# The causal mask of the score bank: written by ScalarE in place of an identity matmul, with the slot order of four engines rewritten

## The reference, cut to what matters

```python
mask = (it < jb) | (it > jb + w) | (jb == -1)
sim = jnp.einsum('bhwie,bhwje->bhwij', bq, bk2) * QK_SCALE
sim = jnp.where(mask, -jnp.finfo(sim.dtype).max, sim)
attn = jax.nn.softmax(sim, -1)
out = jnp.einsum('bhwij,bhwje->bhwie', attn, bv2)
```

## Time and profile before

| what | value |
|---|---|
| median of 3 runs | 3747.72 us (3747.24 to 3754.5) |
| the profiled execution, its own time | 3743.95 us |
| its span | 3742.1 us |
| PE busy | 3470.4 us (93%) |
| PE weight loads busy | 2773.6 us (74%) |
| DVE busy | 3141.4 us (84%) |
| ACT busy | 2271.7 us (61%) |
| POOL busy | 1852.4 us (50%) |

### The profile page before, as it was taken

How to read it: one execution, slowest core, us unless ns; L and a number is a source line. 1 busy time by engine, 2 the same in 40 slices (tenths; PEclk the granted TensorE clock), 3 DMA queues, 4 the chain that set the end, 5 groups by cost and what they waited for, 6 DMA issues and landing times.

```text
span 3742.1 us, 161812 instructions
## 1 busy us (share of the span) xinstructions
PE 3470.4 (93%) x63907; PEld 2773.6 (74%) x63907; DVE 3141.4 (84%) x6016; ACT 2271.7 (61%) x4159; POOL 1852.4 (50%) x1604
## 2 busy tenths in 40 slices
PE   5758999999999999999999999999999999999996
PEld 2326787877788878788878788877788887788784
DVE  8987888888788888788888788888788888888883
ACT  2014666666666666666666666666566666666663
POOL 2435455454554554545554445545455445455541
PEclk9988999999999999999999999999999999999998
DMA  2002423323333323333223333232432332332332
GB/s 84 9 28 50 104 60 70 77 54 78 91 67 77 72 56 80 82 77 77 64 64 76 85 77 71 57 77 67 95 72 59 73 77 54 79 74 60 70 77 73
DMA packets 186363, 261.00 MB, mean 70 GB/s; under 512 B 31670, under 2 KB 89908, under 8 KB 185396
## 3 DMA queue, kind: packets, MB, share of 16 engines
q1 hardware_dynamic: 186164, 258.24, 30.7%
HBM read 22.30 MB, written 4.19 MB: 7 GB/s over the span
## 4 chain that ended last, share of the span: by engine, by line
PE 71%; issue 13%; DVE 7%; POOL 3%; ACT 3%; SPq 2%; DMA 1%; ACTq 0%; POOLq 0%; DVEq 0%
PE bank L653 9%; PE bank L705 8%; PE bank L637 7%; PE bank L613 6%; PE obank L687 6%; PE bank L738 5%; PE bank L615 4%; PE bank L614 4%; PE bank L697 4%; PE bank L663 4%; PE bank L745 3%; DVE xs_lo L1139 3%; PE bank L647 2%; PE bank L628 2%; PE bank L630 2%
## 5 line engine op out<-in xcount | busy, mean ns | idle before, releaser
L951 POOL TENSOR_TENSOR qn<-qn,rinv 128x512 f32<-128x512 f32 x768 | 805.4, 1065 | 1382.1 <-DVE rinv L1198 1382.1
L945 POOL TENSOR_TENSOR qn<-ropec,ropes 128x512 f32<-128x512 f32 x768 | 982.9, 1294 | 274.6 <-DVE ropes L1150 230.8
L1149 DVE TENSOR_TENSOR ropec<-bank,rots 128x512 f32<-128x512 f32 x768 | 526.7, 686 | 116.0 <-ACT sq L833 63.7
L1158 DVE TENSOR_REDUCE ss<-sq 128x8 f32<-128x512 f32 x768 | 513.2, 679 | 88.0 <-ACT sq L833 82.6
L1150 DVE TENSOR_TENSOR ropes<-bank,rots 128x512 f32<-128x512 f32 x768 | 523.7, 682 | 0.0
L833 ACT ACTIVATE sq<-bank 128x512 f32<-128x512 f32 x768 | 448.8, 598 | 87.7 <-PE bank L615 68.9
L855 ACT ACTIVATE Pr<-Pr 128x512 f32<-128x512 f32 x384 | 241.9, 630 | 399.1 <-DVE Pr L1209 396.9
L637 PE MATMUL bank<-ident,qn 128*128 128x128 f32 x3072 | 464.1, 274 | 18.4 <-POOL qn L951 14.9
L653 PEld LDWEIGHTS bank<-kT,qT 64*32 64x32 f32 x24576 | 363.1, 107 | 122.0 <-issue 121.9
L613 PE MATMUL bank<-wqkv_hi,xs_hi 128*128 128x512 f32 x768 | 353.1, 460 | 99.2 <-DVE xs_lo L1139 90.8
L637 PEld LDWEIGHTS bank<-ident,qn 128*128 128x128 f32 x3072 | 375.9, 141 | 83.9 <-issue 18.8
(11 more groups left out here) (137 smaller groups left out, 6215.9 us busy)
## 6 DMA issues: line engine op xcount, KB each, us to landing
V<-Vt SPq DMA_DIRECT2D x576, 260.0 KB
V<-Vt SPq DMA_DIRECT2D x192, 130.0 KB
V<-Vt SPq DMA_DIRECT2D x192, 65.0 KB
xres<-X SPq DMA_DIRECT2D x96, 128.0 KB
X<-x SPq DMA_DIRECT2D x96, 128.0 KB, 2.0
wqkv_raw<-L_ffn_Wqkv SPq DMA_DIRECT2D x6, 1536.0 KB
xraw<-X SPq DMA_DIRECT2D x97, 64.0 KB
xraw<-X SPq DMA_DIRECT2D x97, 63.8 KB
```

What stands on the lines that cost most here:

```text
L945: pool.tensor_tensor(qn[:, c, :], ropec[:, c % ROPE_RING, :], ropes[:, c % ROPE_RING, :], ALU.add).then_inc(rope_sum.sem, 1)
L951: pool.tensor_tensor(heads8(qn[:, c, :]), heads8(qn[:, c, :]), rinv[:, 8 * c:8 * c + 8].unsqueeze(2).broadcast_to([P, 8, DH]), ALU.mult).t ...
L1149: dve.tensor_tensor(halves(ropec[:, c % ROPE_RING, :]), raw, table(t, 2 * kind), ALU.mult)
L1158: dve.tensor_reduce(ss[:, 8 * c:8 * c + 8], heads8(sq[:, c % 2, :]), AX.X, ALU.add).then_inc(ss_done.sem, 1)
```

## The change

The mask matmul of each unit is gone. ACT has a step `mk`: it waits for `sim_shift` and writes the mask in float32 from SBUF over the whole bank with a Copy, then counts `mask_put`. PE waits for `mask_put` before the 32 score matmuls, which all add to what is there. One mask matmul is left, once before the pipeline. The order of all four engines is another one.

```diff
@@ ORDER
     "pe": """
-        tr.0' pt.2'' w1.0''' pv.1'' proj.0 proj.1 tr.1' ot.0'' w1.1''' tr.2' pv.2'' pt.3'' tr.3' proj.2
...
+        proj.0 proj.1 tr.2' pt.3'' w1.1''' tr.3' ot.1'' pv.3'' proj.2 proj.3 tr.4' w1.2''' ot.2'' tr.5'
...
@@ tensor
+            pe.matmul(b_sim[:], identb[:], maskb[:, 0, :].unsqueeze(1).broadcast_to([P, 8, 2 * WIN]),
+                      start=True, stop=True).then_inc(sim_begun, 1)
...
-                pe.wait_ge(sim_shift.sem, sim_shift.at(b, u) if u else sim_shift.at(b - 1, 4))
-
-                pe.matmul(b_sim[:], identb[:], maskb[:, 1 if t else 0, :].unsqueeze(1).broadcast_to([P, 8, 2 * WIN]),
-                          start=True, stop=False, skip_group_check=True)
+                hold(pe, pe_held, mask_put.sem, mask_put.at(b, u + 1))
                 for m in range(8):
@@ scalar
+            act.wait_ge(sim_begun, 1)
+
+            def b_mk(b, u):
+                act.wait_ge(sim_shift.sem, sim_shift.at(b, u) if u else sim_shift.at(b - 1, 4))
+                act.activation(heads8(b_sim[:]), mask_f[:, u // 2, :].unsqueeze(1).broadcast_to([P, 8, 2 * WIN]),
+                               ACT.Copy).then_inc(mask_put.sem, 1)
```

More of the change, by code:

```diff
@@ L52 @@
     "pe": """
-        tr.0' pt.2'' w1.0''' pv.1'' proj.0 proj.1 tr.1' ot.0'' w1.1''' tr.2' pv.2'' pt.3'' tr.3' proj.2
-        proj.3 tr.4' ot.1'' w1.2''' tr.5' pv.3'' proj.4 ot.2'' tr.6' w2.0''' ot.3'' tr.7' proj.5 proj.6
-        qk.0' wo.0'' qk.1' proj.7 v.0 mean.0'' pt.0' qk.2' var.0'' pt.1' pv.0' qk.3' v.1 v.2 ln.0'' v.3 """,
+        proj.0 proj.1 tr.2' pt.3'' w1.1''' tr.3' ot.1'' pv.3'' proj.2 proj.3 tr.4' w1.2''' ot.2'' tr.5'
+        proj.4 ot.3'' tr.6' w2.0''' tr.7' proj.5 proj.6 qk.0' wo.0'' qk.1' proj.7 v.0 mean.0'' pt.0' qk.2'
+        v.1 v.2 var.0'' pt.1' pv.0' qk.3' v.3 ln.0'' pt.2' tr.0 pv.1' w1.0'' ot.0' tr.1 pv.2' """,
     "act": """
-        tr.0' xs.0 wa.1 wa.2 qk.3'' w1.0''' pt.2'' proj.0 tr.1' ot.0'' proj.1 w1.1''' tr.2' pt.3'' tr.3'
-        proj.2 proj.3 tr.4' ot.1'' tr.5' w1.2''' wc.2''' ot.2'' proj.4 tr.6' tr.7' ot.3'' proj.5 proj.6
-        qk.0' x1.0'' wc.0'' proj.7 qk.1' v.0 pt.0' mean.0'' qk.2' v.1 pt.1' v.2 ln.0'' wc.1'' v.3 wc.3''' """,
+        xs.0 wa.1 wa.2 tr.0' qk.3'' w1.0''' tr.1' ot.0'' proj.0 proj.1 tr.2' pt.3'' w1.1''' ot.1'' tr.3'
+        mk.0' proj.2 tr.4' proj.3 w1.2''' wc.2''' ot.2'' tr.5' proj.4 tr.6' ot.3'' tr.7' proj.5 proj.6 mk.1'
+        qk.0' x1.0'' wc.0'' proj.7 mk.2' v.0 mean.0'' qk.1' pt.0' v.1 mk.3' qk.2' v.2 pt.1' v.3 ln.0''
+        wc.1'' pt.2' wc.3''' """,
     "dve": """
-        qk.3'' xs.0 wa.1 wa.2 pv.1'' w1.0''' proj.0 proj.1 sums.0 sums.1 pv.2'' w1.1''' proj.2 proj.3 sums.2
-        w1.2''' sums.3 pv.3'' proj.4 sums.4 w2.0''' sums.5 proj.5 sums.6 qk.0' proj.6 x1.0'' qk.1' sums.7
-        mean.0'' proj.7 qk.2' var.0'' rsqrt.0 pv.0' ln.0'' """,
+        xs.0 wa.1 wa.2 pv.2'' w1.0''' sums.0 sums.1 proj.0 proj.1 w1.1''' pv.3'' proj.2 w1.2''' sums.2
+        sums.3 proj.3 proj.4 w2.0''' sums.4 proj.5 qk.0' proj.6 sums.5 sums.6 x1.0'' qk.1' proj.7 mean.0''
+        sums.7 qk.2' var.0'' rsqrt.0 pv.0' ln.0'' qk.3' pv.1' """,
     "pool": """
-        norm.4' norm.5' add.0 add.1 norm.6' add.2 add.3 norm.7' add.4 norm.0 add.5 norm.1 norm.2 norm.3
-        add.6 add.7 """,
+        norm.6' add.0 add.1 add.2 norm.7' add.3 add.4 norm.0 add.5 norm.1 norm.2 add.6 norm.3 norm.4 add.7
+        norm.5 """,
 }
@@ L201, in build @@
         const_in = sem("const_in")
+        sim_begun = sem("sim_begun")
         x_in_sem = [sem(f"x_in_{k}") for k in range(4)]
@@ L251, in build @@
         max_done = per_batch("max_done", 4)
+        mask_put = per_batch("mask_put", 4)
         sim_shift = per_batch("sim_shift", 4)
@@ L894, in c_ln_ @@
                 act.activation(xn[:], lnt[:], ACT.Identity, bias=vec[:, 1:2], scale=vec[:, 0:1]).then_inc(c_xn.sem, 1)
-            steps = {"xs": a_xs, "proj": a_proj, "v": a_v, "tr": a_tr, "qk": b_qk,
+            steps = {"xs": a_xs, "proj": a_proj, "v": a_v, "tr": a_tr, "mk": b_mk, "qk": b_qk,
                      "pt": b_pt, "ot": b_ot, "x1": c_x1_, "mean": c_mean, "ln": c_ln_,
```

## The result

The changed kernel takes **3652.05 us** (median of 4 runs, 3650.08 to 3656.13) where the kernel before takes 3747.48 (4 runs, 3745.54 to 3754.5): a ratio of **0.9743 [0.9727, 0.976]**, 2.6% faster. The profiled execution took 3651.81, 92 less than the one before.

The account below looks back on a forecast made before the run. PE was taken as the bound: 33.65 us work plus 0.68 wait a loop slot. Saving 1.33 times 67 (89) plus 25 elsewhere, 114, takes 3744.0 to 3630; 3.8 for the median gives 3634 us, range 3592 to 3700.

Parts of the forecast that it names:

- Part 1: Dropping PE's four mask matmuls saves 0.93 us a slot, ends 0.87 and 1.24; entry into tiled scores remains at three.
- Part 2: Mask write on ACT takes 0.60 us, ends 0.4 and 0.9; covered by sum, 0.1 a slot booked for its order.
- the tie: Before the third unit's scores, the turn over DVE and ACT takes 2.43 us against PE's 2.5; 0.1 booked.
- Part 3: PE's wait at `proj.0` for DVE's remainder of x shrinks from 0.68 us to 0.1 to 0.3; the next wait replaces it.
- Part 4: Ring from `tr.0` through PE, the root chain and POOL's first multiplication back takes 32.91 us, 0.2 over PE's work.
- the sum of parts 3 and 4: At the slot seam the remainder-of-x wait gives way to the ring ahead of `tr.0`; loop slot 33.0 us.
- The second ring: Root chain, eight POOL operations, rotary step of `proj.1`, then `proj.3` on PE: 10.6 us against 10.9, slack 0.3, nothing booked.
- The changes of layer: The 28 slots outside the loop gain only the mask, 0.9 each, 25 us; ends 3 us for each of five changes.
- The signs I named: Profile values expected after the change: slot distance 33.0 us, PE's waits, PE busy near 327 in ten slots, block pitches.
- (c): Rival: DVE's shift, late behind rotary pairs, delays ACT's mask write and PE; slower, 3810 us; chance 0.08.
- (a): Rival: all turns and rings covered, PE never stops; loop slot 32.72 us, total 3615; chance 0.15.

Follow-up runs that it names:

- e4: The changed kernel, but ACT writes each mask twice, the second write held until the first is done; 3712.17 us, ratio 0.9888.
- e1: The changed kernel with PE's loop cut between `v.3` and `ln` instead of behind `pv.2`; 3627.27 us, ratio 0.9667.
- e11: The new order with the mask still a matmul on PE and PE's loop cut between `v.3` and `ln`; 3684.34 us, ratio 0.9818.
- e6: e1 with `pv.1` ahead of the first `tr.0` on PE; 3629.03 us, ratio 0.968.
- e7: e6 with DVE's rotary steps of `proj.3` and `proj.4` ahead of the fourth sum of squares; 3615.72 us, ratio 0.9642.
- e9: e7 with DVE's rotary steps of `proj.0` and `proj.1` also ahead of the second sum of squares; 3599.51 us, ratio 0.9597.
- e3: The kernel before, in its old order, with only the mask write moved to ACT; 3889.77 us, ratio 1.0367.
- e5: e3 with ACT's square for the variance ahead of the second exponential; 3790.27 us, ratio 1.0105.
- e12: The changed kernel with PE's loop cut one block earlier, between `tr.1` and `pv.2`; 3638.24 us, ratio 0.9712.
- e8: e1 with PE's loop cut one block earlier, between the last scores and `v.3`; 3633.61 us, ratio 0.9692.
- e10: e9 with `pt.2` ahead of `ln` on PE; 3607.93 us, ratio 0.9624.

## Why the prediction was right, and where it was not

The direction and the main cause were right: PE's own work sets the pace, the mask leaves it, and ACT has room for the writes. The time is 18 us above the forecast.

- **Part 1, the mask matmul.** Forecast 0.93, measured 1.10. The three units behind whole-array work gained 0.21 to 0.23 for my 0.20; the one behind `pv` gained 0.44 for my 0.33. The upper end was 1.24 a slot, which over 95 slots is 29 us and not the 20 that I gave. The mask there cost twice: entering whole-array work after `pv`, and tiles again after it; I had counted one change and there were two. That the change of mode has a price is what the Trainium skill says, page "TensorEngine Tiling (Array Packing)", section Key Properties, and the trace agrees: of the mask's pitches at the first three units (0.32, 0.31, 0.30) 0.09 each came back as entry into the scores, and at the fourth (0.33) 0.11 more than the pitch was gained.
- **Part 2, the mask write.** 0.604 us for the 0.60, a tie in the third unit, room in the others (e4). The page "ScalarE: Activation LUTs" of the Trainium skill, section Step-by-step: what each stage is for, says that ScalarE reaches PSUM faster than SBUF. The runs here don't decide it: the Copy of the mask into PSUM takes 0.604, the exponential from SBUF to SBUF 0.621 (L865) and 0.630 before (L855), copies from PSUM to SBUF 0.586 to 0.597 (L843, L854, L871, L879), and none has one function on one size with either destination. The 0.1 booked for the tie wasn't there.
- **Part 3, the wait for the remainder of x.** It went, entirely.
- **Part 4, the ring through the first transpose.** Right in kind: 0.30 a slot of small waits around `ln` and `tr.0`, 0.37 in e1, and e11 shows what they take from the mask. I had booked 0.2 ahead of `tr`; a third of the 0.30 shows already ahead of `ln`, which waits for the root chain itself, a shorter way round than the one over POOL.
- **The step that failed is the sum of parts 3 and 4**, which let PE run from `pv.2` into `proj.0` without a stop. The list of PE's steps now ends on `pv.2`, and the return of the hardware loop costs 0.39 there. It lies in the ring of part 4 and adds to it. e1 removes it and lands on 33.04 for my 33.0, and on 3627 for my 3634. That it lands so near is in part luck: the mask gave 0.17 more than I had and the 0.1 of the tie wasn't there, while the ring took 0.37 for my 0.2 and a rotary step about 0.1. I had read the seam of the old order, found no stop behind `v.3`, and took that for a property of the seam.
- **The second ring.** Its slack of 0.3 was too large. In the change a rotary step already delays `proj.6` by some 0.15, e6 runs into this ring, and e7 and e9 gain 0.34 a slot by shortening it.
- **The changes of layer.** 30 us from the 28 other slots for 25, 3 of them lost again ahead of the first slot.
- **The signs I named.** The wait before `tr` was to be about 3 us in ten slots and is 3.0, spread over three blocks. PE busy was to be near 327 and is 330.4. The records of `ln` and `tr.0` are longer where these blocks are held up (0.71 and 0.66 for 0.60), so this number contains part of the waits. `pt` before scores was to take 0.56 and takes 0.53; `pv` before scores was to take 0.79 and takes 0.67 (1186.65 to 1187.32). Waits for the mask write were to be about 1 us in ten slots, and there are none. A change of layer stands 18.5 over five loop slots for some 17.
- **Rivals.** (c), slower, did not occur in the change. e3 and e5 show something akin to it in the old order: lateness in ACT's queue, where (c) had it in DVE's, that falls on PE. Most of e3's loss is the clock, which no rival named. (a) at 32.72 a slot is what e9 reaches, with three steps moved.

**What stays open.** How the 0.39 divides between the branch and the sequencer instructions behind it wasn't tried, nor what in the block ahead brings it out. Why PE stops for several us at the cut of its list at a change of layer, and why twice in e12, is not shown; e12 and e8 are 11 and 6 us over e1 with about the same loop slot. What makes the granted clock fall in e3 is open too. e7 and e9 were built on e6, and whether their moves pay as much without it wasn't run. Whether the last 0.1 ahead of `ln` can be had is open; e10 is not the way.

## What to carry to other kernels

When work leaves the busiest engine, add up what is left between each pair of waits, not only the sum: here 1.10 us left PE and 0.73 arrived, because a ring through three other engines became as long as PE's own work. Treat the seam of a loop as a block with a price that depends on the block ahead of it, and try other places for the cut; moving it from behind `pv` to behind the long matmuls of `v.3` changes no work and gave 0.7% here. An engine that has room by its sum may have none at the place of the new step: the same mask write is 2.6% faster with the queues rewritten around it and 1% slower without.
